# Angle attention and graph attention of a graph network: exponentials of a whole 128 x 512 tile on ACT, longer lags, and a mask added by PE

## The reference

```python
def _agnn_layer(h, src, dst, beta, num_nodes):            # angle attention, 4 layers
    h_norm = h * jax.lax.rsqrt(jnp.sum(h * h, axis=-1, keepdims=True) + EPS)
    logits = beta * jnp.sum(h_norm[src] * h_norm[dst], axis=-1)
    m = jax.ops.segment_max(logits, dst, num_segments=num_nodes)
    ex = jnp.exp(logits - m[dst])
    denom = jax.ops.segment_sum(ex, dst, num_segments=num_nodes)
    return jax.ops.segment_sum((ex / (denom[dst] + EPS))[:, None] * h[src], dst, num_segments=num_nodes)

def _gat_layer(x, src, dst, W, a_s, a_d, b):              # graph attention, 3 layers, 4 heads of 64
    h = (x @ W).reshape(n, HEADS, C)
    e = jax.nn.leaky_relu(s_src[src] + s_dst[dst], 0.2)   # s_* = einsum of h with a_s, a_d
    ex = jnp.exp(e - jax.ops.segment_max(e, dst, num_segments=n)[dst])
    alpha = ex / jax.ops.segment_sum(ex, dst, num_segments=n)[dst]
    return jax.ops.segment_sum(h[src] * alpha[:, :, None], dst, num_segments=n).reshape(n, HEADS * C) + b
```

## Time and profile before

| what | value |
|---|---|
| median of 3 runs | 11036.81 us (11017.5 to 11073.92) |
| profiled execution | 11119.13 us, its span 11117.1 us |
| busy in that span | PE 7197.0, DVE 5850.1, POOL 5289.8, ACT 2582.1 us |
| four angle passes | between 4180 and 7740 us |
| three graph attention passes | between 7895 and 11040 us |

### The profile page before, as it was taken

The page is one execution under the profiler, slowest core; times in us unless marked ns, Lnnn a source line. Parts: engine busy times, 40 slices in busy tenths (PEclk is TensorE's granted clock), DMA queues, the critical chain, the costliest instruction groups (busy, mean ns, idle before and its releaser), DMA issues. The chain is left out here.

```text
span 11117.1 us, 155608 instructions
## 1 busy us (share of the span) xinstructions
PE 7197.0 (65%) x34292; PEld 5512.2 (50%) x34293; DVE 5850.1 (53%) x21199; ACT 2582.1 (23%) x6846; POOL 5289.8 (48%) x5498
## 2 busy tenths in 40 slices
PE   0013334434474927886886886887598878887887
PEld 0013334423353826775775775776355545554554
DVE  6012233331113246776666666777576756675767
ACT  0000000000011211221221221221345544544544
POOL 2766666646612125554554554554344434444443
PEclk9986666666667968998998997998666666666666
DMA  3101123343425923353334334334222422232323
GB/s 145 50 14 40 40 54 83 83 68 91 89 19 176 364 89 87 81 80 72 78 79 70 79 79 70 81 80 63 62 69 66 66 62 66 68 60 71 69 68 59
DMA packets 614773, 886.43 MB, mean 80 GB/s; under 512 B 285681, under 2 KB 423153, under 8 KB 613400
## 3 DMA queue, kind: packets, MB, share of 16 engines
q0 software_dynamic: 241344, 609.84, 26.2%
q1 hardware_dynamic: 373336, 275.69, 8.2%
HBM read 757.50 MB, written 134.32 MB: 80 GB/s over the span
## 5 line engine op out<-in xcount | busy, mean ns | idle before, releaser
L1529 POOL DMA_INDIRECT hs<-tab_agnn,rec x1952 | 1899.2, 973 | 1782.6 <-PE psV L1679 655.8
L1963 POOL DMA_INDIRECT hs<-tab_gat,rec x1464 | 1388.1, 948 | 1591.3 <-DVE msg L2032 1156.7
L2139 PE MATMUL psV<-msg,ohf 128*128 128x260 f32 x2928 | 1264.9, 608 | 0.0
L2001 DVE CUSTOM_DVE_ANT_0 cand<-psL,neg 128x512 f32<-128x512 f32 x1464 | 975.6, 685 | 345.7 <-issue 230.9
L1655 PE MATMUL psG<-HN,ohT 128*128 x3904 | 1030.0, 411 | 65.9 <-issue 40.4
L1679 PE MATMUL psV<-hs,pr 128*128 128x258 f32 x3904 | 1056.5, 418 | 5.9 <-DVE pr L1589 5.9
L1550 DVE CUSTOM_DVE_ANT_0 prod<-psG,hs 128x256 f32<-128x256 f32 x1952 | 828.3, 480 | 415.6 <-issue 208.0
L2139 PEld LDWEIGHTS psV<-msg,ohf 128*128 128x128 f32 x2928 | 882.4, 315 | 199.1
L1655 PEld LDWEIGHTS psG<-HN,ohT 128*128 128x128 f32 x3904 | 778.4, 210 | 175.2 <-issue 74.2
L645 PE MATMUL psT<-ident,oh 128*128 128x128 f32 x488 | 120.4, 393 | 1129.0 <-DVE oh L611 1001.7
L1679 PEld LDWEIGHTS psV<-hs,pr 128*128 128x128 f32 x3904 | 752.6, 203 | 106.3 <-DVE pr L1589 8.2
(11 more groups left out here) (324 smaller groups left out, 13041.6 us busy)
## 6 DMA issues: line engine op xcount, KB each, us to landing
w<-in_L_gnn_w SPq DMA_DIRECT2D x224, 512.0 KB, 5.8
fwd_d<-acc SPq DMA_DIRECT2D x10, 3172.0 KB
fw<-fwd_d SPq DMA_DIRECT2D x122, 260.0 KB
hs<-tab_agnn,rec POOLq DMA_INDIRECT x1952
hs<-tab_gat,rec POOLq DMA_INDIRECT x1464
rec<-rec_d SPq DMA_DIRECT2D x1220, 8.0 KB
b<-in_L_gnn_b SPq DMA_DIRECT2D x113, 128.0 KB, 6.5
x<-xbuf SPq DMA_DIRECT2D x112, 128.0 KB, 6.1
```

What stands on the lines that cost most here:

```text
L1529: nc.gpsimd.indirect_dma_start(out=hs[:, j, g, :], out_offset=None, in_=k.tab_agnn, in_offset=bass.IndirectOffsetOnAxis(ap=rec[:, j, g, 0: ...
L1963: nc.gpsimd.indirect_dma_start(out=hs[:, j, g, :], out_offset=None, in_=k.tab_gat, in_offset=bass.IndirectOffsetOnAxis(ap=rec[:, j, g, 0:1 ...
L2001: V.tensor_tensor_reduce(cand[:, m, :], psL[:, m, :], neg[:, h2, :], 1.0, -BIG, ALU.add, ALU.max, mt[:, h2, m:m + 1]).then_inc(s_lt, 1)
L2139: mm = nc.tensor.matmul(psV[:, h4, 0:W_GAT], ohf[:, h4, g, :], msg[:, h4, g, :], start=(g == 0), stop=(g == G - 1))
```

## The change

Angle attention. The weights are made as nodes by edges: `cand` is kept, ACT takes the exponential of the whole tile with the peak as a bias for each node (`prT`, 128 x 512), PE turns it (`psP`, four fp32 transposes), and ACT copies it out (`pr`). `psQ`, `tt`, `below`, `ex` and the four DVE multiplications are gone. The peak is kept with the other sign (`low`, `mn`). The lags are now 0 (`oh`), 1 (`ohT`, `psG`), 2 (`prod`), 3 (`psL`), 4 (`cand`, `prT`, `psP`), 5 (`pr`, `psV`) and 6 (`acc`). `oh` and `ohT` have two buffers where they had six.

Graph attention. PE adds the mask: for each head an identity matmul of `neg` (bf16, 512 columns) and the matmul of the scores, which now has 128 rows, go into one `psL`. DVE takes the maximum of two heads in one instruction. The turned scores take 128 columns in place of 12. The peak's leaky function runs in one instruction with the logits' (`leaky`), ACT copies the peak into `sp`, `below` and the fp32 copy of `oh` are gone, the rows are multiplied in one instruction, and `acc` is scaled in one and added in another. The lags are 0 (`away`), 1 (`psT`, `sT`), 2 (`psL`), 3 (maximum, `psQ`), 4 (`msg`), 5 (`psV`) and 6 (`acc`).

All tables have one more row of zeros, which the padding edges point to; four small DMAs write it before the first stage.

Angle attention:

```diff
+        now, mid_, old, add = (lagged(i, j, n) for n in (0, 2, 4, 6))
...
+            V.tensor_tensor_reduce(cand[:, h4, :], psL[:, :], neg[:, j4 % 3, :], 1.0, -BIG, ALU.add, ALU.max,
...
+            V.scalar_tensor_tensor(out=mn[:, h4:h4 + 1], in0=mt[:, h4:h4 + 1], scalar=-1.0, in1=at,
+                                   op0=ALU.mult, op1=ALU.min).then_inc(q.m, 1)
...
+            V.tensor_tensor(oh[:, j % 2, :, :], mid(k.iota[:, :], G), b3(recf[:, j, :, 1], P),
+                            ALU.is_equal).then_inc(q.oh, 1)
...
+            V.tensor_tensor(df[:, h4:h4 + 1], mn[:, h4:h4 + 1], at, ALU.subtract).then_inc(q.df, 1)
...
+            V.scalar_tensor_tensor(out=acc, in0=acc, scalar=rs[:, j6:j6 + 1], in1=psV[:, 0:cols],
...
+            V.tensor_copy(at, mn[:, h4:h4 + 1]).then_inc(s_mx, 1)
...
+            if not (isinstance(t2, int) and t2 < 2):
+                dve.wait_ge(s_l, own(t2 - 1))
+                dve.wait_ge(q.b, flow(t2 - 1))
...
-            V.tensor_tensor(tt[:, h3, :], lg[:, h3, :], psQ[:, 0:G], ALU.subtract).then_inc(q.tt, 1)
...
-            V.tensor_scalar(below[:, h3, :], tt[:, h3, :], 0.0, None, ALU.min).then_inc(q.min, 1)
...
-                    ins = V.tensor_scalar(pr[:, h3, g, :], oh[:, j3, g, :], ex[:, h3, g:g + 1], None, ALU.mult)
...
+            nc.scalar.activation(ohT[:, j1 % 2, :, :].rearrange("p g e -> p (g e)"), psT[:, :], ACT.Copy).then_inc(s_oT, 1)
...
+            nc.scalar.activation(neg[:, j1 % 3, :], psT[:, :], ACT.Copy, bias=-2 * BIG, scale=2 * BIG).then_inc(q.ev, 1)
...
-            nc.scalar.activation(neg[:, j, :], psT[:, :], ACT.Copy, bias=-BIG, scale=BIG).then_inc(q.ev, 1)
...
+            nc.scalar.activation(prT[:, h, :], cand[:, h, :], ACT.Exp, bias=mn[:, h:h + 1]).then_inc(q.e, 1)
...
+            nc.scalar.activation(rs[:, j4:j4 + 1], df[:, h:h + 1], ACT.Exp).then_inc(q.rs, 1)
...
+            nc.scalar.activation(pr[:, j5 % 2, :, :].rearrange("p g e -> p (g e)"), psP[:, :], ACT.Copy).then_inc(s_p, 1)
+    pipeline(act, step, 5)
...
+        now, last, cos, old, add = (lagged(i, j, n) for n in (0, 1, 3, 4, 5))
...
+            pe.wait_ge(s_l, own(t3) + 1)
+            if not (isinstance(t3, int) and t3 < 1):
+                pe.wait_ge(q.m, flow(t3))
...
+            pe.wait_ge(s_oT, own(t1) + 1)
...
+        if old:
+            _, j4, t4 = old
+            pe.wait_ge(q.e, flow(t4) + 1)
+            if not (isinstance(t4, int) and t4 < 1):
+                pe.wait_ge(s_p, own(t4))
+            for g in range(G):
+                mm = nc.tensor.transpose(psP[:, g * P:(g + 1) * P], prT[:, j4 % 2, g * P:(g + 1) * P], k.ident[:, :])
+            mm.then_inc(s_turn, 1)
...
+        if add:
+            _, j5, t5 = add
+            pe.wait_ge(s_p, own(t5) + 1)
...
-                mm = nc.tensor.matmul(psQ[:, g:g + 1], ohT[:, j2, g, :], mn[:, h2:h2 + 1], start=True, stop=True)
...
+    pipeline(pe, step, 5, numbers=blocks)
```

Graph attention:

```diff
-            mid_, old, add = lagged(i, j, 2), lagged(i, j, 3), lagged(i, j, 4)
+            mid_, old, add = lagged(i, j, 3), lagged(i, j, 4), lagged(i, j, 6)
...
+            def top(pair):
+                if mid_:
+                    m = pair * 2
+                    dve.wait_ge(q.b, spread(t2) + (pair + 1))
+                    V.tensor_reduce(mt[:, h2, m:m + 2], psL[:, m:m + 2, :], AX.X, ALU.max).then_inc(s_lt, 1)
+
+            top(0)
+            top(1)
...
+                V.tensor_tensor(a4, a4, b3(rs[:, j6, :], CH1), ALU.mult).then_inc(s_am, 1)
...
+                V.tensor_tensor(at_block(smax, b), at_block(smax, b), mt[:, h2, :], ALU.max).then_inc(s_mx, 1)
...
+                V.tensor_tensor(raw[:, now, GH:], at_block(smax, b), at_block(sd, b), ALU.add).then_inc(s_mx, 1)
...
+                V.tensor_tensor(g3(raw, now), hrow[:, :, :, C_HEAD], q3[:, :, 0, :], ALU.add).then_inc(s_lg, 1)
...
+                V.scalar_tensor_tensor(out=leaky[:, now, part], in0=raw[:, now, part], scalar=NEG_SLOPE,
+                                       in1=raw[:, now, part], op0=ALU.mult, op1=ALU.max).then_inc(s_leak, 1)
...
+                V.tensor_tensor(g3(t3, h), g3(leaky, now), q3[:, :, 1, :], ALU.subtract).then_inc(q.tt, 1)
...
+                V.tensor_tensor(df[:, h2, :], at_block(peak, b), leaky[:, now, GH:], ALU.subtract).then_inc(q.df, 1)
...
+                V.tensor_tensor(acc, acc, psV[:, j6 % 2, 0:W_GAT], ALU.add).then_inc(q.u, 1)
...
+                V.tensor_tensor(hmsg[:, :, :, 0:C_HEAD], hrow[:, :, :, 0:C_HEAD],
+                                hmsg[:, :, :, C_HEAD].unsqueeze(3).to_broadcast([P, G, HEADS, C_HEAD]),
+                                ALU.mult).then_inc(q.msg3, 1)
...
+            now, last, mid_, old = (lagged(i, j, n) for n in (0, 1, 3, 4))
...
+                    ins = nc.scalar.activation(away[:, j, g, :], k.iota[:, :], ACT.Abs, bias=recf[:, j, g, 1:2], scale=-1.0)
...
+                nc.scalar.activation(flat(oh, h), flat(away, j4), ACT.Relu, bias=1.0, scale=-1.0).then_inc(q.oh, 1)
...
+                nc.scalar.activation(weights, t3[:, h, :], ACT.Exp).then_inc(q.e, 1)
...
+                nc.scalar.activation(at_block(peak, b), leaky[:, j % 2, GH:], ACT.Copy).then_inc(q.m, 1)
...
+                nc.scalar.activation(rs[:, j3, :], df[:, j3 % 2, :], ACT.Exp).then_inc(q.rs, 1)
...
+                nc.scalar.activation(sT[0:PARTS, h1, :], psT[0:PARTS, 1, :], ACT.Copy).then_inc(s_st, 1)
...
+                nc.scalar.activation(flat(ohT, j1 % 3), psT[:, 0, :], ACT.Relu, bias=1.0, scale=-1.0)
+                nc.scalar.activation(neg[:, h1, :], psT[:, 0, :], ACT.Copy, scale=-BIG).then_inc(q.ev, 1)
...
+            last, mid_, low, add = (lagged(i, j, n) for n in (1, 2, 3, 5))
...
+                    nc.tensor.transpose(psT[:, 1, g * P:(g + 1) * P], hsb[:, j1, g, 0:P], k.identb[:, :])
+                    mm = nc.tensor.transpose(psT[:, 0, g * P:(g + 1) * P], away[:, j1, g, :], k.identb[:, :])
...
+            def pair(n):
+                if not (isinstance(t2, int) and t2 < 1):
+                    pe.wait_ge(s_lt, pairs(t2 - 1) + (n + 1))
+                for m in (2 * n, 2 * n + 1):
+                    nc.tensor.matmul(psL[:, m, :], k.identb[:, :], neg[:, h2, :], start=True, stop=False)
+                    mm = nc.tensor.matmul(psL[:, m, :], sel[:, m, :], sT[:, h2, :], start=False, stop=True)
+                mm.then_inc(q.b, 1)
...
-                    nc.tensor.transpose(psT[0:PARTS, 1, g * P:(g + 1) * P], hsb[:, j1, g, 2 * W_GAT:], k.identb[:, :])
...
-                    nc.tensor.matmul(psL[:, m, :], sel[0:PARTS, m, :], sT[:, h1, :], start=True, stop=True).then_inc(q.b, 1)
```

More of the change, by code:

```diff
@@ L1457, in attention_by_angle @@
         psL = ps("psL", [P, G * P])
-        psQ = ps("psQ", [P, 512])
+        psP = ps("psP", [P, G * P])
         psV = ps("psV", [P, 512])
@@ L1609, in step @@
                     def step(i, j):
-                        now, mid_, old = lagged(i, j, 0), lagged(i, j, 2), lagged(i, j, 3)
-                        if old:
-                            _, j3, t3 = old
-                            h = j3 % 2
-                            act.wait_ge(q.min, flow(t3) + 1)
-                            if not (isinstance(t3, int) and t3 < 2):
-                                act.wait_ge(s_p, own(t3 - 1))
-                            nc.scalar.activation(ex[:, h, :], below[:, h, :], ACT.Exp).then_inc(q.e, 1)
@@ L1618, in step @@
-                        if now:
-                            _, _, t = now
-                            act.wait_ge(q.t, flow(t) + 1)
-                            if not (isinstance(t, int) and t < U):
-                                act.wait_ge(q.q, flow(t - U + 1))
-                            nc.scalar.activation(ohT[:, j, :, :].rearrange("p g e -> p (g e)"), psT[:, :], ACT.Copy)
-                            nc.scalar.activation(neg[:, j, :], psT[:, :], ACT.Copy, bias=-BIG, scale=BIG).then_inc(q.ev, 1)
@@ L1625, in step @@
-                        if mid_:
-                            _, j2, t2 = mid_
-                            act.wait_ge(q.df, flow(t2) + 1)
-                            if not (isinstance(t2, int) and t2 < U):
-                                act.wait_ge(q.u, nth(t2 - U + 1))
-                            nc.scalar.activation(rs[:, j2:j2 + 1], df[:, j2 % 2:j2 % 2 + 1], ACT.Exp).then_inc(q.rs, 1)
-                    pipeline(act, step, 3)
+                        last, old, done = (lagged(i, j, n) for n in (1, 4, 5))
@@ L2111, in _ @@
+                        pipeline(act, step, 4, numbers=blocks)
                     @block.tensor
```

446 lines of the change are left out of this document (197 added, 249 removed).

## The result

| | before | after |
|---|---|---|
| median of the runs | 11,043.5 us (4 runs, 11,017.5 to 11,073.9) | 10,719.7 us (4 runs, 10,704.6 to 10,737.2) |
| ratio, 95% interval | | 0.9706, 0.9676 to 0.9737 |
| profiled execution, span | 11,117.1 us | 10,735.1 us |
| granted clock, whole span | 0.771 | 0.806 |

The account below looks back on a forecast made before the run. Bounds: PE waiting on late results in angle attention; DVE's pace and PE's slow clock in graph attention. 11119 - 494 (angle) - 534 (graph) + 50 (drain) = 10,141, set 82 us lower: 10,060 us; range 9,780 to 10,780.

Parts of the forecast that it names:

- I take 5.9, nearest to that pass: Angle attention: step falls from 6.92 to 5.90 us, near the graph convolution pass's 5.81; 494 us off.
- A result of PE is seen late while PE goes on streaming: Angle attention before: `cand` began 2.2 us after `psL` ended, lateness that lands on PE within one step's round trip.
- the loop's head: DVE stands 2.52 us at the head of a loop trip, once in six steps, 0.4 us a step where uncovered.
- rival 2: Angle attention: waits return at `psL` or `psV`, so only PE's work differs; 208 us off, 10,350 us, chance 0.14.
- Graph attention's clock: Graph attention: granted clock rises from 0.67 to about 0.9, step from 8.17 to 6.70 us; 534 us off.
- reductions: Graph attention: two DVE maximum reductions of 1024 elements replace four `cand` of 0.69 us, at 1.22 us each, bounds 1.22 and 1.38.
- half-level step of 10.7: Graph attention: PE's work in a step takes 10.7 us at the half clock level, against 5.90 at full.
- POOL as what is late next: Angle attention: POOL's four gathers, 1.24 us apart, take 5.0 us a step and become the next limit.
- Drain: Pass ends: `acc` comes two groups later, some 7 us for each of seven passes, +50 us.
- ACT's exponential: Angle attention: ACT's exponential of a 512-column tile takes from 0.6 us to twice that, costing nothing beside PE's 4.65.
- Rival 4: Graph attention: clock stays at the half level through the pass; 991 us more, 11,540 us, chance 0.06.
- signs of being wrong: Graph attention's clock below 0.75, `mn` or `pr` heading PE's waits, or DVE's graph attention step over 6.5 us.

Follow-up runs that it names:

- v_one: The changed kernel with `psV`'s sum in angle attention made by one matmul instead of four: 10,594 us, ratio 0.958 to before, on chip 12.
- narrow: The changed kernel with half of each table row gathered in angle attention: 10,761 us, ratio 0.976 to before, on chip 12.
- g_end: The changed kernel with `psG` moved behind `psV` in angle attention: 9,194 us on chip 10; 10,608 us on chip 7 against 10,573 for the changed kernel.

## Why the prediction was wrong

- The step that failed is the one for attention by angle: "I take 5.9, nearest to that pass: 484 x (6.92 - 5.90) = 494 us off". 5.91 is what an undisturbed step takes. The sum had no term for holds and set 5.90 against a mean of before that held 679 us of them. The passes' mean after is 6.80, and the term is 58 us. In the terms of the sum: 315 us for the undisturbed step, and 260 us given back to holds and to the half level. Nor would the term have come true without holds: on chip 10 the angle's part alone lost 143 us, and the kernels with both parts are some 500 us under before, half of the forecast, all of it from graph attention.
- The reading under it: "A result of PE is seen late while PE goes on streaming", from the earlier trace rows. I took the 2.2 us of `cand` for a property of each round trip, and the 2.52 us behind it for the loop's head. But ACT stood there as well, for a `psT` that had ended at 4515.95:

```profile
4515.56 0.39 PE L1664 MATMUL psT<-identb,oh 128*128 128x128 bf16 x4
...
4520.00 0.60 ACT L1623 ACTIVATE ohT<-psT 128x512 f32<-128x512 bf16 x1 [7.99 <-remote]
```

  In the semaphore events the increments of `psG`, `psT`, `psQ` and `psV` come between 4519.91 and 4520.16, for matmuls that ended from 4515.7 to 4519.7. The trace of before has 112 holds in the angle passes, 5.8 us long in the mean. Looking at one stretch I saw one engine's wait, and not that all of PE's increments, and with them all engines, stood together.
- "The lags do not help angle attention" was rival 2, at 0.14, with 208 us for it. That is the nearest to what happened in effect, but not by its mechanism: neither `mn` nor `pr` heads PE's waits, `ohT` does. The gain was smaller still, 58 us.
- Graph attention's clock of "about 0.9": 0.87. The reductions "1.22 each": 1.22. Its undisturbed step 6.24 against PE's 5.90; the half-level step of 10.7 can't be checked by these rows (10.26 or 8.06, by the line that counts). With 150 holds on top the step is 7.08, not 6.70, 138 us, and 70 more come from setting the gain against 8.17 and not 7.98.
- POOL as what is late next, with steps near 5.0 to 5.8: right on chip 10, where its gathers fill the time; in the first trace of after it was idle ahead of its gathers for 1,714 us of the angle passes, 397 of them behind increments of `psV` and 442 behind a releaser that the profile could not place.
- Drain: +50 forecast. From a pass's last group of `prod` to the next pass's first it is 66.5 us after and 65.7 before, and from `psV` to `psV` some 4 us more between those of graph attention: 10 us in all.
- PE's clean step 4.65: 4.62. ACT's exponential, bounded from 0.6 to twice that, took 0.72.
- Rival 4's sum is 45 us short: 10,060 + 534 + 991 is 11,585, not 11,540. Nothing hangs on it.
- None of the signs of being wrong came: the clock in graph attention was 0.87, neither `mn` nor `pr` headed PE's waits, and DVE was busy 626 of 880 us, 5.1 a step. None of them asked how long an increment stays unseen.

What stays open: why TensorE's increments are held, why one chip of four has none, and what in a faster pace brings it on. The holds don't go with less of its work (v_one), nor with half of the bytes gathered (narrow), nor with another place of `psG` (g_end). Nor is it settled why the angle's part loses on chip 10.

## What to carry to other kernels

When several engines start within a microsecond after a wait whose releaser had long ended, look at the producer's increments over a whole pass before calling it a round trip: count how often it happens and what share of the time it takes, and give it a term in the sum. A stage that is close to TensorE's own step may gain little from being made denser (58 us here), and on such a chip four idle memsets a step even gained 97. And run the kernel before beside the changed one on every chip: the same code took a fifth less time a step in the angle passes on one of them, and a sixth less in graph attention.
